# Two transposes ahead of the row addition in an LSTM step, and another engine for the last store

## The reference

```python
x = x + _L0_gnn_ref(_layernorm(x), edge_index, W1, b1, W2, b2)
def step(carry, x_t):
    h_prev, c_prev = carry
    combined = jnp.concatenate((x_t, h_prev), axis=1)
    f_t = sigmoid(combined @ W_f + b_f)
    i_t = sigmoid(combined @ W_i + b_i)
    c_t = f_t * c_prev + i_t * tanh(combined @ W_c + b_c)
    o_t = sigmoid(combined @ W_o + b_o)
    h_t = o_t * tanh(c_t)
    return ((h_t, c_t), h_t)
x = x + scan(step, _layernorm(x))
```

## Time and profile before

| | us |
|---|---|
| median of 3 runs | 2661.74 (2660.68 to 2664.11) |
| the profiled execution's own time | 2665.65 |
| its span | 2664.1 |
| PE busy in the span | 2514.0 (94%) |
| DVE busy | 2156.0 (81%) |
| ACT busy | 1560.6 (59%) |
| POOL busy | 998.1 (37%) |

### The profile page before, as it was taken

The page is one execution under the profiler, slowest core; times in us unless marked ns, Lnnn a source line. Parts: engine busy times, 40 slices in busy tenths (PEclk is TensorE's granted clock), DMA queues, the critical chain, the costliest instruction groups (busy, mean ns, idle before and its releaser), DMA issues. The chain is left out here.

```text
span 2664.1 us, 47528 instructions
## 1 busy us (share of the span) xinstructions
PE 2514.0 (94%) x10745; PEld 1830.3 (69%) x10746; DVE 2156.0 (81%) x5780; ACT 1560.6 (59%) x3989; POOL 998.1 (37%) x1018
## 2 busy tenths in 40 slices
PE   7978999999999999999979999999998999989997
PEld 5865777777777777777756666666665556555554
DVE  7757888888888898888848877777777777778786
ACT  5655555555555555555536656666665777767775
POOL 1127777777777767777520000000000000023333
PEclk9997999999999999999989999999999999999998
DMA  9647998898988888888777747777777666499995
GB/s 236 189 134 230 296 277 253 263 278 257 276 267 267 264 246 279 274 257 264 232 208 199 195 121 237 244 237 237 236 243 209 167 168 169 137 235 251 252 250 144
DMA packets 194207, 611.15 MB, mean 229 GB/s; under 512 B 41822, under 2 KB 47966, under 8 KB 164394
## 3 DMA queue, kind: packets, MB, share of 16 engines
q1 hardware_dynamic: 120432, 370.08, 46.8%
q0 software_dynamic: 73712, 240.39, 31.7%
HBM read 468.71 MB, written 141.62 MB: 229 GB/s over the span
## 5 line engine op out<-in xcount | busy, mean ns | idle before, releaser
L834 POOL DMA_INDIRECT kept<-ln_table,kept x800 | 822.7, 1028 | 291.8 <-issue 208.4
L1548 PE MATMUL acc<-shared,state 128*125 128x512 f32 x2244 | 775.3, 416 | 63.5 <-DVE state L1867 48.8
L1548 PEld LDWEIGHTS acc<-shared,state 128*125 128x125 f32 x2244 | 401.6, 187 | 198.1 <-ACT acc L1477 67.6
L875 ACT ACTIVATE shared<-kept 128x512 fp32r<-128x512 f32 x800 | 441.3, 624 | 152.2 <-PE agg L928 109.4
L1387 POOL TENSOR_TENSOR out<-h,lx 125x512 f32<-125x512 f32 x50 | 64.5, 1290 | 1107.7 <-DVE h L1892 1107.7
L928 PE MATMUL agg<-shared,onehot 128*125 128x512 f32 x1200 | 377.4, 408 | 21.7 <-DVE shared L1045 18.6
L1548 PE MATMUL acc<-W_low,state 128*125 128x512 f32 x800 | 316.5, 396 | 0.0
L1548 PE MATMUL acc<-last_high,state 128*125 128x512 f32 x748 | 298.7, 399 | 0.0
L928 PEld LDWEIGHTS agg<-shared,onehot 128*125 128x125 f32 x1200 | 225.5, 189 | 98.5 <-DVE low_part L1045 16.8
L1045 DVE TENSOR_TENSOR low_part<-kept,shared 128x512 fp32r<-128x512 f32 x400 | 265.7, 693 | 10.8 <-ACT shared L875 4.3
L1045 DVE TENSOR_TENSOR shared<-kept,shared 128x512 fp32r<-128x512 f32 x400 | 259.3, 688 | 16.3 <-ACT shared L875 10.5
(11 more groups left out here) (237 smaller groups left out, 4379.4 us busy)
## 6 DMA issues: line engine op xcount, KB each, us to landing
xg<-total_rows SPq DMA_DIRECT2D x100, 896.0 KB
xg<-gate_rows SPq DMA_DIRECT2D x88, 896.0 KB
gate_rows<-gout SPq DMA_DIRECT2D x200, 224.0 KB
total_rows<-total SPq DMA_DIRECT2D x50, 896.0 KB
kept<-ln_table,kept POOLq DMA_INDIRECT x800, 4.5
lx<-x_rows POOLq DMA_DIRECT2D x50, 250.0 KB, 7.3
out_dram<-out POOLq DMA_DIRECT2D x50, 250.0 KB, 2.9
held<-in_x_dram SPq DMA_DIRECT2D x25, 448.0 KB
```

The costliest lines, as they stand in the source:

```text
L834: e.indirect_dma_start(out=rows[j % RING][:, :], out_offset=None, in_=table[:, :], in_offset=bass.IndirectOffsetOnAxis(ap=ends[:, b, j, 0: ...
L875: e.activation(high[j % PARTS][:, :], rows[j % RING][:, :], ACT.Copy).then_inc(s_high, 1)
L1548: m = e.matmul(acc[n][0:L, :], stationary[:, k, :], weights[k][:, n * PAIR:(n + 1) * PAIR], start=begins, stop=(k == K - 1), skip_group_ch ...
```

## The change

On TensorE, in the change and final rounds, transposes 0 and 1 now stand ahead of the row addition, and the products begin with bank 0: (0,0), (2,0), transpose 2, (0,1), transpose 3, (1,0), (1,1), then the rest. ScalarE's seeds of acc0 and acc1 change places, with the semaphore values to match. The last step's output rows are stored by SyncE instead of GpSimd, with a semaphore of their own (s_y_last), and GpSimd executes a drain right behind its last addition, ahead of its last waits.

```diff
@@ SyncE @@
+                if kind in ("final", "more"):
+                    hold(e, s_passed, s_out, (r - FINAL) * STEPS + (STEPS + AHEAD))
+                    e.dma_start(y_v[STEPS - 1], out[(STEPS - 1) % 2][0:L, :]).then_inc(s_y_last, 16)
@@ GpSimd @@
                     if not buffer_new:
-                        e.wait_ge(s_y[par], (stored - par) * 8)
+                        e.wait_ge(s_y[par], (r - FINAL) * ((STEPS // 2 - par) * 16) + (s - par) * 8)
...
                                     x1[par][0:L, :], ALU.add).then_inc(s_out, 1)
+                    if last:
+                        return
                     hold(e, s_passed, s_out, stored + (AHEAD + 1))
                     e.dma_start(y_v[s], out[par][0:L, :]).then_inc(s_y[par], 16)
...
                     step(STEPS - 2 + par, par, last=(par == 1))
+                if kind == "final":
+                    e.drain()
+                hold(e, s_passed, s_y_last, (r - FINAL + 1) * 16)
                 for par in range(2):
-                    hold(e, s_passed, s_y[par], (r - FINAL + 1) * (STEPS // 2 * 16))
+                    hold(e, s_passed, s_y[par], (r - FINAL + 1) * ((STEPS // 2 - par) * 16))
@@ ScalarE @@
                         output_gate(1)
+                        seed(0)
+                        new_cell(SECOND)
                         seed(1)
-                        new_cell(SECOND)
-                        seed(0)
@@ TensorE @@
                         else:
-                            e.wait_ge(s_seed, SEEDED + (r - CHANGE) * (2 * (STEPS - 1)) + (s - 1) * 2 + (2 - n))
+                            e.wait_ge(s_seed, SEEDED + (r - CHANGE) * (2 * (STEPS - 1)) + (s - 1) * 2 + (n + 1))
...
                         else:
+                            turn_before(0)
+                            turn_before(1)
                             if not first:
                                 add_rows(2)
-                            turn_before(0)
-                            turn_before(1)
+                            seeded(0)
+                            product(0, 0)
+                            product(2, 0)
+                            turn_before(2)
+                            product(0, 1)
+                            turn_before(3)
                             seeded(1)
-                            product(1, 0)
-                            product(2, 0)
-                            product(1, 1)
-                            turn_before(2)
-                            turn_before(3)
-                            seeded(0)
-                            for k in range(K):
+                            for k in FIRST:
+                                product(1, k)
+                            for k in SECOND:
                                 product(0, k)
```

More of the change, by code:

```diff
@@ L1235, in lstm_part @@
         s_y = [sem(ctx, f"s_y{n}") for n in range(2)]
+        s_y_last = sem(ctx, "s_y_last")
         s_clear = sem(ctx, "s_clear")
```

## The result

The changed kernel takes **2652.87 us** (median of 6 runs, 2650.33 to 2653.37) against 2662.87 us for the kernel before (6 runs on the same chip): a ratio of 0.9963, 95% interval 0.9953 to 0.9973, or 10.0 us. The forecast was 2652.5.

A forecast was written before the change was run, and what follows sets the result against it. It took a step to be a cycle through several engines, TensorE 91% busy yet waiting for VectorE's state. Steps -4.4 and -0.5, end -4.3, sum -9.2 us: 2652.5 against the median 2661.74; 8 in 10 range 2641 to 2661.

The forecast's parts named there:

- Part 1, transposes ahead: TensorE's transposes before the row addition: state 0 comes 0.21 us earlier per change step, 0.13 per final step.
- No slack: The addition and two products just fit between transpose 1 and transpose 2; 0.02 us a step was charged.
- Part 2, bank 0 first: Product (0,1) between transposes 2 and 3 makes state 3 0.14 us late; cost 0.10 us a step, range 0.03 to 0.23.
- The k=3 product: Sign in a step: bank 0's k=3 product 1.25 to 1.30 us behind transpose 2's load instead of 1.17.
- Net: Steps' total: -0.09 us per change step, -0.01 per final step, 49 steps each, -4.9 us together.
- The addition as the wall: Rival, 12%: the addition between h1 and transpose 2 overruns and delays every step; +5.5 us, 2667.2 us.
- Part 3, the end: GpSimd's early drain at the kernel's end overlaps its last waits: -4.3 us, bounds -3.8 and -4.6.
- The rival that the drain is a fixed price: Rival, 10%: GpSimd's 8.3 us drain is paid again behind the check, end +3.1 us, 2656.8 to 2660 us.
- The sum: Whole kernel: -4.4 and -0.5 us in the steps, -4.3 at the end, -9.2 us together.

The follow-up runs named there:

- e2: The change with the row addition still ahead of the transposes (new end and bank 0 first kept): 2667.35 us, ratio 1.0015 to the kernel before.
- e10: The change with the row addition cut into two column halves, start flag on the first alone, the change's order behind: 2937.06 us, ratio 0.9966 to the kernel before.
- e5: The change without GpSimd's early drain: 2655.52 us, ratio 0.9973 to the kernel before.
- e8: The change with one more GpSimd drain halfway through the final round's steps: 2651.05 us in one run.
- e11: The change itself again, timed beside the two split-addition kernels: 2937.84 us, ratio 0.9965 to the kernel before.
- e1: The kernel before with only the new end (SyncE's last store, GpSimd's early drain): 2659.25 us, ratio 0.9983 to the kernel before.
- e4: The change with bank 1 first and the seeds as before (transposes ahead of the addition and new end kept): 2658.18 us, ratio 0.9981 to the kernel before.
- e9: The change with the row addition in two column halves, one start flag, bank 1 first as in the kernel before: 2927.64 us, ratio 0.9923 to the kernel before.
- e12: e9 run once more beside the kernel before: 2948.22 us, ratio 0.9932 to the kernel before.
- e6: The change with the row addition in two column halves, start flag on both, bank 1 first as in the kernel before: 5471.17 us, ratio 2.055 to the kernel before.
- e7: The change with the row addition in two column halves, start flag on both, the change's bank 0 first: 5480.09 us, ratio 2.059 to the kernel before.

## Why the prediction was right

**Part 1, transposes ahead: right in size, given part 2.** It said -0.21 and -0.13, plus 0.02 for want of slack. From e2 to the change, which differ in this alone, the periods fall by 0.20 and 0.11 us. The distances it named came out: 0.49 us to state 0, and the addition's load at 2417.33, 0.17 us behind transpose 1's.

**No slack: true, and free.** Transpose 2's matmul did start 0.03 to 0.05 us late, as charged. But e10, where it doesn't, has the same gate. The 0.02 should have been 0.

**Part 2, bank 0 first: right.** It charged 0.10 us; e2 measures 0.09 in both rounds. Transpose 3's matmul stands 0.36 us behind transpose 2's (0.33 foretold). The k=3 product is recorded 1.19 us behind transpose 2's load, but with 0.46 us in place of 0.39, so it ends at 1.65 where it was 1.56, as if it began at 1.26 (1.25 to 1.30 foretold; by the recorded start alone this sign didn't come). Of the 0.14 us by which state 3 is later, 0.05 are covered, as the working had it: before, the k=3 product stood 0.15 us behind its load, held by the products and not by the state. The 0.10 was picked from a range of 0.03 to 0.23; 0.14 less the cover of 0.05, both in the working, gives the measured 0.09.

**Net.** -0.12 and -0.02 us against -0.09 and -0.01; -6.7 us over the rounds for -4.9, less 0.8 lost once between the rounds, which nobody foresaw and no run explains (that distance is 22.3 to 22.5 us in the change, e5, e8, e10 and e11, and 20.8 to 21.9 in the kernel before, e1 to e4, e9 and e12).

**Where the text misled, though the sum held.** It priced the two parts as if each stood alone. e4 says otherwise: part 1 without part 2 gives -0.04 and +0.04, not -0.19 and -0.11. The working did count two products between the addition and transpose 2, which is the changed order, so the pair was priced rightly, but not the parts. The addition as the wall was a rival at 12%; it is what e4 shows, with one product more. Its remark that TensorE's idle time moves to where h0 is awaited came true: 22.1 us of it stand there.

**Part 3, the end: -4.8 instead of -4.3.** The 8.3 us came as forecast (8.2 behind the addition). Its bounds for the second drain were 0 and 1.47 us; it took 0.13, so the near end was right. GpSimd's check and branch were put at 1.1 us and took 1.5 (2647.30 to 2648.77), so that it came last by 0.1 us after all; TensorE's branch took 3.59 us instead of 3.90, without which the end couldn't have fallen below the nearer bound. The rival that the drain is a fixed price is refuted by e8, which halves it: the earlier trace rows, e5 and e8 have 8.29, 8.21 and 4.2 us behind some 100, 100 and 50 DMAs, and a drain with none since the last takes 0.13. A price for each DMA isn't shown, though: 396 took 5.4 us in e6 and some 820 took 13.5 in the earlier trace rows. The rule that the prediction set against part 3 (the Trainium skill, "VectorE: DVE Perf Modes", section "The DRAIN you can't avoid") gives some 12 ns to the runtime's boilerplate drains of preamble and postamble. The drain at this kernel's block end is the program's own, and only SyncE's (7 ns) was that short. Read as the prediction did, the rule makes nothing of part 3, and that was wrong by 4.8 us.

**The sum** was -9.2; the medians say -10.0, with an interval of 0.001 to either side (2.7 us), and the LSTM's time -11.0.

## What to carry to other kernels

Find the one handover that a step hangs on, and list everything that must come before it on each engine. A move in such a row is worth what the later of its two limits gives, so parts of a change are priced together, in the new order; work that fits nowhere whole may fit in two halves, in two waits. A drain of an engine that issues its own DMAs, GpSimd here, can cost microseconds; put it where the engine has nothing to do. And an accumulation that is cut by columns inside one PSUM bank is started once.

## What the runs showed of the hardware

- GpSimd's drain took 8.2 to 8.3 us with some 100 of its DMAs since the last drain, 4.2 with half of them, and 0.13 with none; but 5.4 with 396 (e6, e7). It is recorded from its issue, so the row also holds the operation that still ran.
- A start flag reaches beyond the columns that its matmul writes: e6 and e9 differ in this flag alone, and 5471 us against 2928 is the difference.
- The kernel before took 2662 to 2663 us in the first three comparisons and 2946 and 2968 in the last two, the chip's or the moment's doing. The chip's number alone doesn't decide it: 2663 us (beside e1 to e4) and 2968 us (beside e12) are both recorded for chip 1. All of it lies in the first half. Of the same stretch of the graph part, e11's row follows the change's:

```profile
600.00:1000.00 400.00, 399.25 (x1771) 311.64 (x1770) 356.98 (x688) 220.12 (x462) 292.88 (x281) 1.00 0.85 262
```

```profile
600.00:1000.00 400.00, 349.20 (x1447) 272.19 (x1445) 287.69 (x556) 177.53 (x374) 242.40 (x232) 0.93 0.73 216
```

  TensorE was busy for 399 us of 400 there, and is so for 349 at a granted clock of 0.93 (a mean over the stretch), with less traffic. Which came first, slower transfers or the clock, no run here tells; the steps of the LSTM agree to 0.01 us.
